# Attention of a two-layer block: softmax sums inverted through DRAM and multiplied in a turn later, values of two head groups in one projection

## The reference

```
q, k, v = x @ Wq, x @ Wk, x @ Wv          # (b, 1024, 16 heads, 16)
s = q @ k.T / 4, masked causally          # per head
p = softmax(s)                            # exp(s - max) / sum
out = (p @ v) @ Wo
```

## Time and profile before

| | |
|---|---|
| median of 3 runs | 2411.98 us (2408.28 to 2419.59) |
| the profiled execution | 2414.42 us, of which the span of the profile is 2412.6 us |
| PE / PEld busy | 2034.7 us (84%) / 1386.3 us (57%) |
| DVE, ACT, POOL busy | 1599.6, 856.7, 446.7 us |
| first attention | from about 43 to 437 us of the span |
| second attention | from about 1717 to 2131 us |

### The profile page before, as it was taken

One profiled execution on the slowest core, in us unless ns is written; L12 is line 12 of the kernel. 1 busy time (PEld: TensorE's weight loads), 2 busy tenths in 40 slices (PEclk: granted clock), 3 DMA queues, 4 the chain that ended last, 5 costly groups with the idle time before them and its releaser, 6 DMA issues. The chain is left out here.

```text
span 2412.6 us, 32196 instructions
## 1 busy us (share of the span) xinstructions
PE 2034.7 (84%) x11288; PEld 1386.3 (57%) x11288; DVE 1599.6 (66%) x3514; ACT 856.7 (36%) x1599; POOL 446.7 (19%) x324
## 2 busy tenths in 40 slices
PE   7899999699999989757766385646689999999998
PEld 4466665388888867334433242323356666469997
DVE  3677773254544355779999999995567777246775
ACT  2255554122223222431112111111335555435775
POOL 0011110423333030001001100110001010105775
PEclk9699999799999999878887698868879999989999
DMA  4111110211110010200000000000121211018886
GB/s 158 42 36 38 44 35 10 83 57 53 52 52 17 0 53 1 86 1 9 9 3 7 18 9 9 0 0 18 36 47 35 47 36 29 9 37 255 235 234 125
DMA packets 52448, 122.19 MB, mean 51 GB/s; under 512 B 14224, under 2 KB 25232, under 8 KB 49488
## 3 DMA queue, kind: packets, MB, share of 16 engines
q1 hardware_dynamic: 42704, 107.40, 14.9%
q0 software_dynamic: 8832, 12.16, 2.9%
q10 hardware_dynamic: 768, 0.79, 0.1%
HBM read 84.09 MB, written 10.52 MB: 39 GB/s over the span
## 5 line engine op out<-in xcount | busy, mean ns | idle before, releaser
L672 DVE CUSTOM_DVE_ANT_0 a_junk<-pair,a_mask 128x512 f32<-128x512 f32 (+3 forms) x768 | 394.2, 551 | 188.1 <-PE pair L519 184.5
L633 ACT ACTIVATE a_prob<-pair 128x512 f32<-128x512 f32 (+3 forms) x768 | 329.0, 496 | 306.5 <-PE pair L543 303.4
L543 PE MATMUL pair<-a_qx,a_kx 98*128 98x512 f32 (+3 forms) x768 | 266.0, 393 | 6.8 <-ACT a_prob L633 6.7
L519 PE MATMUL pair<-a_kx,a_qx 96*128 96x512 f32 (+3 forms) x768 | 246.2, 391 | 22.7 <-DMA a_qx<-a_comp 17.9
L475 POOL TENSOR_SCALAR_AFFINE_SELECT a_prob<-a_prob 128x512 f32<-128x512 f32 x128 | 81.2, 635 | 700.2 <-ACT a_prob L633 700.2
L903 DVE TENSOR_TENSOR m_h<-pair,m_g 128x512 f32<-128x512 f32 x96 | 66.3, 691 | 211.3 <-PE pair L726 210.2
L1285 PE MATMUL pair<-h_stream,r_w_kz 128*128 128x512 f32 x192 | 103.9, 695 | 118.5 <-DVE r_region L1691 113.3
L724 PE MATMUL pair<-m_x_hi,m_w_lo 128*128 128x512 f32 x448 | 178.1, 398 | 26.5 <-POOL m_w_lo L788 24.4
L519 PEld LDWEIGHTS pair<-a_kx,a_qx 96*128 96x128 f32 x768 | 150.6, 204 | 70.4 <-DVE a_mx_raw L672 28.2
L543 PEld LDWEIGHTS pair<-a_qx,a_kx 98*128 98x128 f32 x768 | 143.0, 193 | 74.4 <-ACT a_prob L633 39.3
L725 PE MATMUL pair<-m_x_hi,m_w_hi 128*128 128x512 f32 x448 | 176.8, 395 | 0.0
(11 more groups left out here) (305 smaller groups left out, 4254.7 us busy)
## 6 DMA issues: line engine op xcount, KB each, us to landing
mx_raw<-in_L_ffn_experts SPq DMA_DIRECT2D x69, 512.0 KB, 4.9
m_raw<-in_L_cond_experts SPq DMA_DIRECT2D x18, 1024.0 KB, 4.8
a_kx<-a_comp SPq DMA_DIRECT2D x96, 128.0 KB, 2.4
a_qx<-a_comp SPq DMA_DIRECT2D x360, 32.0 KB, 2.0
r_w_ring<-in_r_q_w SPq DMA_DIRECT2D x8, 512.0 KB, 3.9
m_raw<-in_L_cond_experts SPq DMA_DIRECT2D x6, 512.0 KB, 3.4
token_rows<-mx_h_rows SPq DMA_DIRECT2D x2, 1040.0 KB, 8.1
x_stream<-in_x SPq DMA_DIRECT2D x1, 2048.0 KB, 10.6
```

What stands on the lines that cost most here:

```text
L519: nc.tensor.matmul(first_bank[t % FR][:, 0:c1 - c0], qx[0:PRODUCT, m % 2, a, i * P:(i + 1) * P], kx[0:PRODUCT, m % 3, a // 2, c0:c1], star ...
L543: nc.tensor.matmul(score_bank[t % SR][:, q0:TT], kx[0:ROWS, n % 3, a // 2, j * P:(j + 1) * P], qx[0:ROWS, n % 2, a, h * TT + q0:(h + 1) * ...
L633: nc.scalar.activation(prob[:, i % RING, a, q0:TT], score_bank[t % SR][:, q0:TT], ACT.Exp, scale=SCALE).then_inc(s["b_exp"], 1)
L672: nc.vector.tensor_tensor_reduce(out=junk[:, t % 2, 0:cols], in0=first_bank[t % FR][:, 0:cols], in1=mask[:, m0:m0 + cols], scale=1.0, scal ...
```

## The change

1. Groups 0 to 6 no longer use `sums` and `spread`. ACT copies the value product straight into `a_o_all`. SP stores the sums of the group to DRAM (`norm` step 0), loads them back as 64 x 64 values (step 1), DVE inverts these (step 2), SP stores the inverses to DRAM (step 3) and loads them as a tile `a_factor` of 128 x 1024, each head's row broadcast over its 32 partitions, in four DMAs (step 4). DVE multiplies `a_o_all` in place by it, 128 x 1024, in step 2 of the turn after (step 5). Group 7 keeps `sums` and `spread`.
2. One value projection makes half the tokens of two groups: the weight columns hold 64 channels of one group and 64 of the next. There is one such item in each of the turns 0 to 5 (step 6), where there were two in each of the turns 0 to 6; `a_v` has four buffers, and DVE copies in two instructions per item.
3. The maximum writes its full output back to the PSUM bank that it reads, and the scrap tile and a wait on the second last maximum are gone. The mask tile is 640 columns wide instead of 1024.
4. Between the recurrent branch and the last branch stands one more `end_layer`, which clears the semaphores and joins all engines at a barrier.

The core of the diff:

```diff
-SMALL = (("max", 0, 1), ("sums", -1, 1), ("spread", -1, 1), ("qk", 2, 0), ("qk", 2, 1), ("max", 1, 0),
-         ("v", 1, 0), ("v", 1, 1), ("sums", 0, 0), None, None, ("spread", 0, 0))
+SMALL = (("max", 0, 1), None, None, ("qk", 2, 0), ("qk", 2, 1), ("max", 1, 0), ("v", 0, 0), None, None, None, None, None)
+NORM = {2: 0, 3: 1, 6: 2, 7: 3, 9: 4}
+NORM_LAST = {1: 0, 2: 1, 4: 2, 5: 3, 6: 4, 8: 5}
...
+            if (i, a) == (2, 0) and n > 1:
+                order.append(("norm", n - 2, 5))
...
+        norm = (NORM_LAST if closing else NORM).get(i)
+        if n and norm is not None:
+            order.append(("norm", n - 1, norm))
...
+                def norm(n, step):
+                    group = slice(n * HALF, (n + 1) * HALF)
+                    if step == 0:
+                        sp.wait_ge(s["o_cp"], (n + 1) * HALF)
+                        sp.dma_start(totals[n, :, :], o_all[HD:P:SLOT, group, :].rearrange("p h t -> p (h t)"))\
+                            .then_inc(s["n_out"], 16)
+                    elif step == 1:
+                        sp.wait_ge(s["n_out"], (n + 1) * 16)
+                        if n:
+                            sp.wait_ge(s["n_rcp"], n)
+                        sp.dma_start(total[:, :, :], totals[n, :, :].rearrange("a (p c) -> p a c", p=64)).then_inc(s["n_in"], 16)
+                    elif step == 3:
+                        sp.wait_ge(s["n_rcp"], n + 1)
+                        sp.dma_start(inverses[n, :, :].rearrange("a (p c) -> p a c", p=64), inverse[:, :, :])\
+                            .then_inc(s["n_back"], 16)
+                    elif step == 4:
+                        sp.wait_ge(s["n_back"], (n + 1) * 16)
+                        if n:
+                            sp.wait_ge(s["n_done"], n)
+                        for a in range(GH):
+                            sp.dma_start(factor[a * SLOT:(a + 1) * SLOT, :], inverses[n, a:a + 1, :].broadcast_to([SLOT, T]))\
+                                .then_inc(s["n_wide"], 16)
...
-                    if m * NF + t >= 2:
-                        dve.wait_ge(s["a_max"], m * NF + t - 1)
                     nc.vector.tensor_tensor_reduce(
-                        out=junk[:, t % 2, 0:cols], in0=first_bank[t % FR][:, 0:cols], in1=mask[:, m0:m0 + cols],
+                        out=first_bank[t % FR][:, 0:cols], in0=first_bank[t % FR][:, 0:cols], in1=mask[:, m0:m0 + cols],
...
+                def norm(n, step):
+                    if step == 2:
+                        dve.wait_ge(s["n_in"], (n + 1) * 16)
+                        if n:
+                            dve.wait_ge(s["n_back"], n * 16)
+                        nc.vector.reciprocal(inverse[:, :, :].rearrange("p a c -> p (a c)"), total[:, :, :].rearrange("p a c -> p (a c)"))\
+                            .then_inc(s["n_rcp"], 1)
+                    elif step == 5:
+                        dve.wait_ge(s["n_wide"], (n + 1) * GH * 16)
+                        tile = o_all[:, n * HALF:(n + 1) * HALF, :].rearrange("p h t -> p (h t)")
+                        nc.vector.tensor_tensor(tile, tile, factor[:, :], ALU.mult).then_inc(s["n_done"], 1)
...
         recurrent(c, A)
+        c.end_layer()
+
         last_branch(c, A, rows, out)
```

More of the change, by code:

```diff
@@ L234 @@
                 (2, 1, 0, 2), (2, 0, 1, 0), (1, 1, 2, 0), (1, 2, 0, 0))
-SMALL = (("max", 0, 1), ("sums", -1, 1), ("spread", -1, 1), ("qk", 2, 0), ("qk", 2, 1), ("max", 1, 0),
-         ("v", 1, 0), ("v", 1, 1), ("sums", 0, 0), None, None, ("spread", 0, 0))
-SMALL_LAST = (("max", 0, 1), ("sums", -1, 1), ("out", 0, 0), ("spread", -1, 1), ("out", 0, 1), ("out", 1, 0),
+SMALL = (("max", 0, 1), None, None, ("qk", 2, 0), ("qk", 2, 1), ("max", 1, 0), ("v", 0, 0), None, None, None, None, None)
+SMALL_LAST = (("max", 0, 1), None, ("out", 0, 0), None, ("out", 0, 1), ("out", 1, 0),
               ("sums", 0, 0), ("spread", 0, 0), ("out", 1, 1), ("out", 2, 0), ("out", 2, 1), None)
+NORM = {2: 0, 3: 1, 6: 2, 7: 3, 9: 4}
+NORM_LAST = {1: 0, 2: 1, 4: 2, 5: 3, 6: 4, 8: 5}
 def cut(h, j):
@@ L317, in turn @@
             what, x, y = small
-            entry = (what, x, y) if what == "out" else (what, n + x, y)
-            if 0 <= entry[1] < NG:
+            if what == "out":
+                entry = (what, x, y)
+            elif what == "v":
+                entry = (what, n // 2 + 1, n % 2)
+            else:
+                entry = (what, n + x, y)
+            if entry[1] < (NG // 2 if what == "v" else NG):
                 order.append(entry)
@@ L455, in _ @@
                         place_maxima(*which)
+                    elif what == "norm":
+                        norm(*which)
                     elif what == "split" and which == [NG - 1, 1]:
@@ L496, in qk_projection, with v_projection @@
                     last.then_inc(s["proj"], 1)
-                def v_projection(m, v):
-                    bank = take("v", m, v)
+                def v_projection(pair, v):
+                    m = 2 * pair
+                    bank = take("v", pair, v)
                     for t in range(4):
@@ L551, in values @@
                     if i == 0:
[L552 removed]
+                        pe.wait_ge(s["used"], used("v", n // 2, 1))
                     if j >= 4 * h:
@@ L558, in values @@
                         r = quadrant(a)
-                        last = nc.tensor.matmul(value_bank[r, q0:TT], v_sb[:, n % 2, j, r], prob[:, i % RING, a, q0:TT],
+                        last = nc.tensor.matmul(value_bank[r, q0:TT], v_sb[:, n % 4, j, r], prob[:, i % RING, a, q0:TT],
                                                 start=j == 0, stop=j == 4 * h + 3)
@@ L567, in sums @@
                     for i in range(TT // P):
-                        last = nc.tensor.matmul(bank[:, i * GH:(i + 1) * GH], o_raw[:, h, i * P:(i + 1) * P],
+                        last = nc.tensor.matmul(bank[:, i * GH:(i + 1) * GH], o_all[:, n * HALF + h, i * P:(i + 1) * P],
                                                 c.sum_pick[:, :], start=True, stop=True)
@@ L587, in out_projection @@
                     b, h = t // HALF, t % HALF
-                    pe.wait_ge(s["used"], used("spread", b * GROUPS + GROUPS - 1, h))
+                    pe.wait_ge(s["n_done"], (b + 1) * GROUPS - b)
+                    if b == B - 1:
+                        pe.wait_ge(s["used"], used("spread", NG - 1, h))
                     bank = take("out", t, o)
@@ L637, in copy_result @@
                     act.wait_ge(s["pv"], n * NS + (4 if h == 0 else NS))
[L638 to L640 removed]
+                    nc.scalar.activation(o_all[:, n * HALF + h, :], value_bank, ACT.Copy).then_inc(s["o_cp"], 1)
                 does = {"qk": upper, "q_slots": place_first_queries, "scores": probabilities, "copy": copy_result}
@@ L656, in lower, with copy_values @@
                         .then_inc(s["used"], 1)
-                def copy_values(m, v):
-                    dve.wait_ge(s["vp"], m * 2 + v + 1)
-                    nc.vector.tensor_copy(
-                        v_sb[:, m % 2, 4 * v:4 * v + 4, :].rearrange("p t (a s) -> p (t a) s", s=SLOT)[:, :, 0:HD],
-                        bank_of("v", m, v).rearrange("p (x s) -> p x s", s=SLOT)[:, :, 0:HD])\
-                        .then_inc(s["used"], 1)
+                def copy_values(pair, v):
+                    dve.wait_ge(s["vp"], pair * 2 + v + 1)
+                    for x in range(2):
+                        last = nc.vector.tensor_copy(
+                            v_sb[:, (2 * pair + x) % 4, 4 * v:4 * v + 4, :].rearrange("p t (a s) -> p t a s", s=SLOT)[:, :, :, 0:HD],
+                            bank_of("v", pair, v).rearrange("p (t x a s) -> p t x a s", t=4, x=2, s=HD)[:, :, x, :, :])
+                    last.then_inc(s["used"], 1)
                 def maximum(m, t):
@@ L715, in _ @@
                 does = {"qk_use": lower, "v_use": copy_values, "first": maximum, "split": split_maxima, "max_use": copy_maxima,
-                        "sums_use": reciprocals, "spread_use": divide, "out_use": add_result}
+                        "sums_use": reciprocals, "spread_use": divide, "out_use": add_result, "norm": norm}
                 for what, *which in ORDER:
@@ L2565, in _column @@
     return v.reshape(-1, P).T
-def _slots(w):
-    out = np.zeros((w.shape[0], GROUPS, GH, SLOT), w.dtype)
-    out[..., :HD] = w.reshape(w.shape[0], GROUPS, GH, HD)
-    return out
 def _qkv(wq, wk, wv):
     compact = [w.reshape(D, GROUPS, GH * HD) for w in (wq, wk)]
-    parts = [np.concatenate(compact, 2), _slots(wv).reshape(D, GROUPS, P)]
+    values = np.zeros((D, GROUPS, P), wv.dtype)
+    values[:, 0::2] = wv.reshape(D, GROUPS // 2, P)
+    parts = [np.concatenate(compact, 2), values]
     return np.stack([w.reshape(KD, P, GROUPS, P).transpose(1, 2, 0, 3) for w in parts], 2)
```

33 lines of the change are left out of this document (16 added, 17 removed).

## The result

The changed kernel took 2354.75 us (median; 2350.18 to 2359.97), the kernel before in the same series 2411.39. The ratio is 0.976, with a 95% interval from 0.973 to 0.979: 2.4% faster. The profiled execution took 2359.97 us, 54.4 less than the profiled one of before. The forecast of 2355 us came out. Its sum doesn't hold in that form: the stall that it puts at step 4 isn't there, another of nearly the same size stands elsewhere, and a loss of 3 us in each of three stretches was not foreseen.

The account below looks back on a forecast made before the run. It took PE's stream to bound the 41.1 us turns, then SP's round. Profiled 2414.4 us, less 82.2 from PE, plus 20.3 of waits at step 4, 1.0 for DVE and 1.0 for the barrier: 2354.5, say 2355; range 2330 to 2385.

Parts of the forecast that it names:

- the stall that it puts at step 4: PE waits there for the maxima's DMA: 1.75 us in turns 2 to 5, 3.15 in turn 6, 20.3 in all.
- What goes from PE: Both attentions: `sums`, `spread` and half the value projections leave PE's stream, saving 82.2 us, 5.6 in a middle turn.
- The rival in which these matmuls weren't on the path: The matmuls taken out of PE's stream were not on the path, leaving 2415 us; chance 0.04.
- SP's round: SP's chain from step 4 of one turn to step 4 of the next: 37.25 us, longer than PE's 35.5.
- the hop: SP's store of the inverses, until it has landed in DRAM: 2.2 us.
- Queries and maxima: SP's issue of these loads ahead of step 4, read from turn 3 of the kernel before: 11.31 us.
- I add 1 us in all: DVE, steps 10 to 2: allowance because the multiplication and the splits leave it little air, 1 us in all.
- I take no difference: DVE's maximum writing PSUM in place of the scrap tile costs nothing extra, staying at about 683 ns for 128x512.
- The clock still 1.00: Expected sign in the profile after: the clock stays at 1.00.
- SP keeps ahead: Rival: everything new on SP is hidden, turns of 35.5 us, 2333 us, up to 2338 if DVE binds; chance 0.17.
- The dear round trip: Rival: the store to DRAM takes 4.9 us, making 2381 us, up to 2400 with slow issues; chance 0.12.
- The two bounds by DVE: Rivals: DVE falls behind in part, 2375 to 2410 us, chance 0.07; slow PSUM writes, 2475 to 2505, chance 0.05.

Follow-up runs that it names:

- norm_only: Changed kernel with the value projection as it was before the change (one group at a time, two halves a turn): 2377.13 us, ratio 0.9862.
- no_return_dmas: Changed kernel without the store of the inverses and the four broadcast loads, the factors a constant 1: 2350.66 us, ratio 0.9751.
- mult_late: Changed kernel with DVE's multiplication behind the small item of step 6 instead of in step 2, turns 2 to 6: 2353.5 us, ratio 0.9764.
- scrap_in_sbuf: Changed kernel with the maximum's scrap output back in an SBUF tile in the first attention only: 2351.07 us, ratio 0.9759.
- The repairs: Four changed-kernel variants: multiplication on GpSimd 2355.01 us; late multiplication, one broadcast load 2367.71; GpSimd, one load, early output projection 2350.97; that plus SBUF scrap 2354.49.
- all_and_scrap: Changed kernel with multiplication on GpSimd, one broadcast load, last turn's output projection earlier, and first attention's maximum scrap in SBUF: 2354.49 us, ratio 0.9754.
- late_one_load: Changed kernel with the multiplication behind step 6's small item in turns 2 to 5 and one broadcast load for four: 2367.71 us, ratio 0.9811.
- out_early: Changed kernel with the last turn's output projection tiles in steps 1, 2, 4, 5 instead of 2, 4, 5, 8: 2352.41 us, ratio 0.9765.

## Why the prediction was right, and where it was not

**What goes from PE: right.** `norm_only` and the changed kernel differ by 1.65 us a turn for the projection taken at 1.81. The rival in which these matmuls weren't on the path is refuted by every turn. Only `spread` was worth a little less than its price, which is worked out below.

**SP's round: the step that failed.** Four of its terms held: 6.16 us from step 4 to the keys was 6.16 (219.77 to 225.93), the hop 2.03 for 2.2, the loads 2.33 for 2.49; keys, queries and maxima took 14.0 in turn 2 for 13.81 (15.3 in turn 3, whose six key issues took 5.18). "Queries and maxima: 219.05 to 230.36, 11.31" failed. It was read off a turn in which twelve issues took 8.47 us and four 2.80; in turn 3 they now take from 207.49 to 217.49, 10.0. From step 4 of turn 2 (182.57) to the landing of turn 3's maxima (217.49 and 1.18) it is then 36.1 us, 1.1 less than the turn, and step 4 waits for the maxima's DMA only in turn 6, for 0.44 us in place of 3.15. `no_return_dmas` shows that the 37.2 us don't come from SP.

**DVE: mis-sized.** "I add 1 us in all" and "I take no difference" stood where most of the 1.7 us in each middle turn (37.2 for 35.5) belonged. The multiplication's price (1.22, measured 1.21) was right, and so was the remark that it would hold up the maxima queued behind it, but I had tied that to late loads. It holds them up anyway, because ahead of step 4 DVE has no air, and PE's wait at step 4 that was to cover it didn't exist. Of the 1.7 us 0.9 to 1.0 are the multiplication (turn 1 without it has 11.31 us ahead of step 4, turn 2 has 12.23, and `mult_late` has 11.5 and 11.3 in turns 2 and 3). The maximum into PSUM is 0.035 us on 512 columns and 0.25 to 0.45 of the turn.

The rest, about 0.3 us, is mostly `spread`. I had priced it from its own start, 228.32 to 229.31, 0.99 us. It has to be priced from the start of the value product in front of it, once with it (before) and once without it (turn 1 of the changed kernel):

```profile
227.65 0.85 PE L559 MATMUL pair<-a_prob,a_v 128*32 128x384 f32 x8
228.32 1.06 PE L578 MATMUL pair<-ident,a_o_rcp 128*32 128x128 f32 x32
229.31 0.33 PE L543 MATMUL pair<-a_qx,a_kx 98*128 98x128 f32 x1
```

```profile
141.00 0.85 PE L601 MATMUL pair<-a_prob,a_v 128*32 128x384 f32 x8
141.78 0.33 PE L585 MATMUL pair<-a_qx,a_kx 98*128 98x128 f32 x1
...
142.98 0.47 PE L561 MATMUL pair<-a_kx,a_qx 96*128 96x512 f32 x1
```

That is 1.66 us against 0.78: the item was worth 0.88, and it goes twice in a turn. In turn 3 the parts add up. From the value product of step 1 to that of step 2 it has 3.65 us (211.84 to 215.49), turn 1 has 2.63 (138.37 to 141.00): 1.02 for the multiplication. With 0.41 for the maxima and 0.22 for `spread` that is 1.65 of the 1.70.

Turn 1 of the changed kernel also shows what comes next. Its 11.31 us ahead of step 4 are 0.44 more than 12.77 - 1.90. About 0.11 of that is `spread` and 0.18 the maximum into PSUM. The last 0.15 is a wait for queries too short for the list of waits: SP issues the twelve from 134.01 to 141.49, and 1.49 us after that, at 142.98, the first score in the last row above starts.

```profile
134.01 7.48 SPq L451 DMA_DIRECT2D a_qx<-a_comp  x12
```

`scrap_in_sbuf` confirms it. In its turn 1 DVE is busy for 9.63 us of this stretch instead of 10.31, PE comes to that score earlier, waits, and step 4 is again 11.31 us behind the turn's start. So once the multiplication is out of the way, the chain of release, twelve issues, landing and score sets 11.31 us, and a turn of 36.3 us with the 24.96 behind step 4. That chain is SP's, but it lies inside a turn and goes through the queries, not through the maxima at step 4. The repairs ran into it.

So a term that was too large by 1.7 us and others that were too small by as much stood in the same sum. The errors cancelled, which was luck, and only the experiments tell them apart.

**Turn 7 and the clock: missed.** "The clock still 1.00" held in 11 of 14 turns. The last turns were to save 1.9 us each and saved nothing, and turn 1 of the second attention took 3 us longer than that of the first. With the 1.3 us that the second attention's last turn lost on top these are 8 us (2 x 1.9, 1.3 and 3.1), more than the 5.5 us by which the profiled execution lies above the sum. At a clock of 1.00 the last turn's stretch to step 4 has 12.68 us, so 1.2 of the 1.9 would have been saved; the half clock costs 2.85. The same two waits, of 0.44 and 0.63 us, stand in 18 last turns of the kernels traced, and the clock fell behind them in 9.

**The rivals.** That SP keeps ahead came true as a mechanism, yet not at 2333 us, since DVE took its place at 37.2 us rather than 35.5. The dear round trip didn't show: the store in 64-byte pieces took 2.03 us. With the Trainium skill's figure of about 2.0 us for a DMA's fixed part (DMA: Bandwidth & Descriptors, Anatomy of one DMA, given there for DMAs that GpSimd issues) this trace agrees for SP's. Its rule on pieces under 512 B (Specifications) left no mark that this kernel can show. The two bounds by DVE had the right engine: a maximum longer by 0.14 or 0.22 us would have decided them, and it was 0.035.

## What to carry to other kernels

An engine with a sixth of its time idle over a turn may have none in the stretch where another waits for it: before work is added to it, look at its busy share between the two points where it is waited for, not over the loop. The price of an item in a stream is the distance from the start of what stands in front of it to the start of what follows, with the item less without it. When a chain of a queue is summed up, take each term's shortest and usual value, and not the pass at hand, which may be long because the queue had time. A forecast that comes out proves its total alone; the rows that it named (here a wait at step 4) have to be there too.

## What the runs showed of the hardware

- The granted clock can fall to 0.50 behind short waits of PE in a stream that is otherwise full. Behind waits of 0.44 and 0.63 us it fell in 9 of the 18 last turns that have both. Behind waits for queries it fell after 1.32 us (`mult_late`, turn 4) and 1.50 (the changed kernel, second attention), and stayed at 1.00 after 1.76 us in turn 2 of `all_and_scrap`'s second attention and in turn 3 of `late_one_load`'s. Waits of 0.91 alone, once in a turn, left it at 1.00 everywhere. So the length of a wait alone doesn't decide; what does is open. In a last turn the half clock costs 2.85 us (15.53 for 12.68); a spell of 3.4 us costs about 1.6 (turn 1 of the second attention to its step 4: 14.54 us in `no_return_dmas` with one, 12.94 in `out_early` without, behind the same wait).
- With its output in PSUM the maximum of 512 columns takes 718 ns (683 to SBUF) and the read of its accumulator 138 ns (82). The latter overlaps the next instruction: from maximum to maximum it is 0.65 us for 0.61.
- A multiplication of 128x1024 by GpSimd (2.35 us) held a cast of 16 columns on DVE for 2.31 us.
- One load that writes 512 KB took 9.7 us, four of 128 KB each 2.7 us (median). Why the one took so long is open.
- Twelve issues of equal loads took from 7.5 us to between 8.4 and 9.1 us on SyncE, turn by turn, in every kernel.
